# Identity matmuls on TensorE while it waits at the start of a graph-attention layer

## The chip, the cores and the metric

The kernel runs on one core of a Trainium2 chip. The metric is the device time of one execution in microseconds; a measurement is the median of a few executions. TensorE (PE) multiplies matrices, VectorE (DVE), ScalarE (ACT) and GpSimd (POOL) do the element-wise work, and SyncE (SP) issues most of the DMAs. Each engine runs its own list of instructions in order and waits on semaphores that others raise.

## The reference

One layer of masked attention and an MLP over 128 graphs of 64 nodes, 512 channels, 8 heads, everything in float32:

```
nx = layernorm(x, ln1_g, ln1_b)
q, k, v = nx @ Wq + bq, nx @ Wk + bk, nx @ Wv + bv          # 512 x 512 each
scores = where(adj, q k^T / 8, -1e9);  attn = softmax(scores)
x = x + (attn v) @ Wo + bo
nx = layernorm(x, ln2_g, ln2_b)
return x + gelu(nx @ W1 + b1) @ W2 + b2                     # 512 -> 2048 -> 512
```

## The kernel before

The 8192 tokens are worked off in 16 groups of 512 tokens (4 tiles of 128). The first phase does the attention group by group. The second phase does the MLP over 8 super groups of 1024 tokens. Float32 products of the linear layers are split into three matmuls of a rounded type (`split3`, lines 180 to 182): weights and activations each have a high part (`w_hi`, `nxT_hi`) and a low part (`w_lo`, `nxT_lo`), and hi*lo, lo*hi and hi*hi are summed in PSUM. Each of these matmuls has 512 columns. Scores, attention outputs and transposes use plain float32 operands.

The start is written out by hand, and the change is there. Every engine has a list of its own for it:

- GpSimd fills the 128x128 identity matrix `ident` (lines 530 to 533) and raises `ident_done`.
- SyncE loads the four tiles of the first group of `x`, then `Wq` in four parts, `Wk`, `Wv`, the second group of `x` and the first mask.
- VectorE takes statistics of one tile after another (line 936 and after it), GpSimd takes the power that gives the reciprocal root (line 666), and VectorE normalizes the tile (line 957), raising `zn_done`.
- TensorE waits for `ident_done`, then for each tile for `zn_done`, and transposes its four 128x128 blocks with the identity (line 1539), 16 transposes in all, into four PSUM banks that are otherwise those of the scores and of the transposed probabilities. The last tile's four raise `t_done` one by one.
- ScalarE turns each of the four transposed blocks into `z1T` (scale and bias, line 700) and rounds it to `nxT_hi` (line 707). VectorE subtracts to get `nxT_lo` (line 980) and raises `nx_split`. ScalarE also rounds the weights (lines 689 and 887), and the low parts of the weights are made by VectorE (lines 927 and 1292) and, for `Wk`, by GpSimd (line 661).
- TensorE then makes the queries of the first group (`first_queries`): for each of 4 chunks of the channels it waits for `nx_split` and issues 12 matmuls of 512 columns, 48 in all, into the four banks `lin[0]` to `lin[3]`. After them it makes the keys, which need `wk_lo`, the values, which need `wv_lo`, and the transposes of the second group (line 1351).

After the start, TensorE's work follows `ORDER`, a hand-written list for one group of the first phase: S are scores (line 1398), P transposes of probabilities (line 1408), O attention outputs (line 1425), W output projections, U linear units of the next group. The last group has a list of its own, `LAST_ORDER`, in which the first products of the MLP stand between pieces of attention; around 790 and 817 us the trace is in the last two groups.

In PSUM, `lin` has `LIN` = 4 banks of 128 x 512 float32. The first matmul of each accumulation group overwrites its bank (start=True).

Of the kernel before, what the change touches and what calls it, by code (L numbers as in the profile page):

```python
# [38 lines left out]
P = 128  # L39
# [7 lines left out]
TILES = 4  # L47
# [23 lines left out]
LIN = 4  # L71
# [41 lines left out]
def order_of(g):  # L113
    if isinstance(g, int) and g < 0:
        units = [("U", j) for j in FIRST_UNITS]
        return units[:-3] + [("T", k) for k in range(KC)] + units[-3:] if g == -1 else []
    if is_last(g):
        return LAST_ORDER
    if isinstance(g, int) and g == NG - 2:

        return [("S", 0), ("U", 0), ("U", 1), ("U", 3), ("P", 0), ("U", 4), ("U", 6), ("S", 1), ("O", 0), ("U", 7), ("W", 0),
                ("P", 1), ("U", 9), ("O", 1), ("W", 1), ("U", 10), ("W", 2), ("W", 3)]
    return [(k, n) for k, n in ORDER if k in kinds_of(g)]
# [38 lines left out]
def is_first(g):  # L162
    return isinstance(g, int) and g == 0
# [21 lines left out]
def adj_layer(nc, x_dram, adj, ln1_g, ln1_b, ln2_g, ln2_b, wq, bq, wk, bk, wv, bv, wo, bo, w1, b1, w2, b2, out_dram):  # L185
# [10 lines left out]
    with ctx:  # L196
# [8 lines left out]
        ident = sb("ident", [P, P])  # L205
# [15 lines left out]
        start = nc.sbuf_base  # L221
# [66 lines left out]
        with ExitStack() as phase:  # L288
            lin_banks = phase.enter_context(nc.psum_tensor("lin", [P, LIN, GT], F32))
            lin = [lin_banks[:, i] for i in range(LIN)]  # L290
# [1036 lines left out]
        def _(pe):  # L1327
            def take_bank(g, kind, n):

                bank, last = ring_place(g, kind, n)  # L1330
                if last is not None:
                    i, kind, n = last
                    which = {"U": (q_done, k_done, v_done)[n % 3], "L": v_done, "T": nx_done, "O": att_split,
                             "W": x1_done}[kind]
                    if kind == "L":
                        pe.wait_ge(v_done, KC * i + n // 3 + 1)
                    elif kind == "U":
                        pe.wait_ge(which, KC * (i + 1) + n // 3 + 1)
                    elif kind == "T":
                        pe.wait_ge(which, KC * (i + 2) + n + 1)  # L1340
                    elif kind == "O":
                        pe.wait_ge(which, PAIRS * i + n // 2 + 1)
                    else:
                        pe.wait_ge(which, TILES * i + n + 1)
                return lin[bank]

            def transposes(g, par, k, bank):

                pe.wait_ge(zn_done, TILES * (g + 1))
                for t in range(TILES):  # L1350
                    mm = pe.transpose(bank[:, t * P:(t + 1) * P], x[par][:, t, k * P:(k + 1) * P], ident[:, :])
                mm.then_inc(t_done, 1)

            def unit(g, j, bank):

                m, which = j // 3, j % 3
                if is_first(g) and m == 0:
                    pe.wait_ge(w_lo_done[which], 1)
                for c in range(KC):
                    if j == 0:  # L1360
                        pe.wait_ge(nx_split, KC * g + c + 1)
                    nx = (nxT_hi[:, c, :], nxT_lo[:, c, :])
                    if which < 2:
                        lhs = tuple(w[which][:, c, m * P:(m + 1) * P] for w in (w_hi, w_lo))
                        rhs = nx
                    else:
                        lhs = tuple(n[:, m * P:(m + 1) * P] for n in nx)
                        rhs = tuple(w[2][:, c, :] for w in (w_hi, w_lo))
                    mm = split3(pe, bank[:, :], lhs, rhs, c == 0, c == KC - 1)
                mm.then_inc(u_done, 1)  # L1370
# [13 lines left out]
            def score(g, par, u):  # L1384


                n = PAIRS * g + u
                if u == 0:
                    pe.wait_ge(q_done, KC * (g + 1))
                    pe.wait_ge(k_done, KC * (g + 1))  # L1390
                wait_apart(pe, masked, n, s_passed)
                for t in range(2):
                    for m in range(KC):
                        for a in range(2):
                            at = (2 * u + t) * P + a * NODES
                            for h in range(2):
                                rows = slice(h * HD, (h + 1) * HD)
                                mm = pe.matmul(ps_scores[a * NODES:(a + 1) * NODES, h * KC + m, t, :],
                                               qT[par][rows, m, at:at + NODES], kT[par][rows, m, at:at + NODES],
                                               start=True, stop=True)  # L1400
                mm.then_inc(s_done, 1)

            def prob_transposes(g, u):
                n = PAIRS * g + u
                pe.wait_ge(prob_done, n + 1)
                wait(pe, probT_done, 4 * n)
                for h in range(HEADS):
                    mm = pe.transpose(ps_probT[:, h, :], prob[:, h, :, :], ident[:, :])
                mm.then_inc(pt_done, 1)
# [29 lines left out]
            def body(g, par):  # L1439
                for kind, n in order_of(g):  # L1440
                    if kind == "S":
                        score(g, par, n)
                    elif kind == "P":
                        prob_transposes(g, n)
                    elif kind == "F":
                        product(0, 0, n)
                    elif kind == "L":
                        unit(g, n, take_bank(g, "L", n))
                    elif kind == "U":
                        if is_first(g + 1) and n % 3 == 0:  # L1450
                            if n == 0:
                                first_queries()
                        else:
                            unit(g + 1, n, take_bank(g, "U", n))
                    elif kind == "O":
                        attend(g, par, n, [take_bank(g, "O", 2 * n + a) for a in range(2)])
                    elif kind == "W":
                        project(g, n, take_bank(g, "W", n))
                    else:
                        transposes(g + 2, par, n, take_bank(g, "T", n))  # L1460


            def product(s, q, i):

                n = NQ * s + q
                if i == 1:
                    pe.wait_ge(w1_loaded[q % 2], 16 * (NQ // 2 * s + q // 2 + 1))
                if q == 0:
                    pe.wait_ge(conv_split, PROD * s + CONV.index(i) + 1)
                first_step = isinstance(s, int) and s == 0 and q == 0  # L1470
                if i == 1:
                    if first_step:
                        pe.wait_ge(masked, PAIRS * NG)
                    else:
                        pe.wait_ge(gelu_done["C21"], n)
                elif i == 2:
                    if first_step:
                        pe.wait_ge(probT_done, 4 * PAIRS * NG)
                    else:
                        pe.wait_ge(c_added["C11"], n)  # L1480
                elif i == 5:
                    if not first_step:
                        pe.wait_ge(c_added["C12"], n)
                elif i == 3:
                    pe.wait_ge(c_added["C22"], n + 1)
                else:
                    pe.wait_ge(snap_done[{6: 0, 7: 1, 4: 2}[i]], n + 1)
                for c in range(2):
                    mm = split3(pe, ps_of[i][:, :],
                                tuple(w1_ring[:, q % 2, part, W_AT[i], c * P:(c + 1) * P] for part in range(2)),  # L1490
                                tuple(nxc[:, NX_AT[i], part, c] for part in range(2)),
                                c == 0 and i in (1, 2, 5), c == 1, i not in (1, 2, 5))
                mm.then_inc(p_done[i], 1)
# [39 lines left out]

            pe.wait_ge(ident_done, 1)

            for t in range(TILES):
                pe.wait_ge(zn_done, t + 1)
                for k in range(KC):
                    mm = pe.transpose(first_t[k][:, t * P:(t + 1) * P], x[0][:, t, k * P:(k + 1) * P],
                                      ident[:, :])  # L1540
                    if t == TILES - 1:
                        mm.then_inc(t_done, 1)
            body(-1, 1)
            body(0, 0)
            with pe.Fori(1, NG - 4, 2) as g:
# [36 lines left out]
```

## Time and profile before

| | us |
|---|---|
| median of 3 executions | 2147.41 |
| lowest and highest of them | 2147.28, 2148.95 |
| the profiled execution, whole | 2148.58 |
| its span, first to last instruction on the core | 2146.6 |
| TensorE busy in the span | 2125.0 |
| VectorE busy | 1490.7 |
| ScalarE busy | 905.0 |

The profiled execution is 1.17 us above the median, and 1.98 us of it lie outside the span. All times below are from the start of the span. In the timeline, a matmul's duration includes its way through the engine, so neighbouring matmuls overlap; what tells the pace of a stream is the distance from one start to the next.

### The profile page before, as it was taken

The page shows a single profiled execution, that of the slowest core. Times are in us where ns is not written, and L with a number is a line of the kernel's source. Part 1 is how long each engine was busy: PE and PEld are TensorE (multiplying, and loading weights), DVE is VectorE, ACT ScalarE, POOL GpSimd, SP SyncE. Part 2 cuts the span into 40 slices and gives each one's busy share as a digit, 9 for nine tenths or more (in the row PEclk, how much of TensorE's full clock was granted, in tenths as well). Part 3 has the DMA queues.
Part 4 walks back from the last instruction along what each step waited for, and adds up shares of the span by engine and source line. Part 5 has one row for each costly group of instructions (what it writes and reads, how often), then busy time and mean ns, then how long its engine had stood idle before and what let it go on. Part 6 is the DMA issues. An engine that isn't in the chain of part 4 may idle for free.

```text
span 2146.6 us, 33138 instructions
## 1 busy us (share of the span) xinstructions
PE 2125.0 (99%) x13216; PEld 1754.3 (82%) x13216; DVE 1490.7 (69%) x2211; ACT 905.0 (42%) x1321; POOL 431.6 (20%) x293
## 2 busy tenths in 40 slices
PE   8999999999999999999999999999999999999999
PEld 6888888888888877888888888888888888888887
DVE  5888888888999966666666666666666656666333
ACT  4444444433344444435335335335345345345332
POOL 2233434321111224004004004003003003003200
PEclk9999999999999999999999999999999999999999
DMA  6344333431222116336445445444444544544532
GB/s 188 111 155 135 134 134 134 146 117 66 70 76 70 46 56 231 150 140 223 170 156 206 168 173 190 177 181 179 187 181 171 196 180 167 201 165 172 211 129 92
DMA packets 103842, 323.98 MB, mean 151 GB/s; under 512 B 21409, under 2 KB 29601, under 8 KB 87329
## 3 DMA queue, kind: packets, MB, share of 16 engines
q1 hardware_dynamic: 98192, 321.68, 40.9%
q8 instruction: 85, 1.39, 0.3%
q10 hardware_dynamic: 5520, 0.55, 0.2%
q14 instruction: 45, 0.36, 0.1%
HBM read 265.57 MB, written 56.62 MB: 150 GB/s over the span
## 4 chain that ended last, share of the span: by engine, by line
PE 96%; DVE 3%; DMA 0%; ACT 0%; issue 0%; POOL 0%; SPq 0%; DVEq 0%; ACTq 0%
PE lin L180 11%; PE lin L182 10%; PE lin L181 10%; PE ps_r L180 5%; PE ps_r L182 5%; PE ps_r L181 5%; PE ps_x L180 5%; PE ps_x L182 5%; PE ps_out L182 5%; PE ps_x L181 5%; PE ps_out L181 5%; PE ps_out L180 5%; PE ps_z L182 3%; PE ps_z L181 3%; PE ps_z L180 3%; PE lin L1425 1%
## 5 line engine op out<-in xcount | busy, mean ns | idle before, releaser
L1209 DVE TENSOR_TENSOR acc<-ps_r,acc 128x512 f32<-128x512 f32 x256 | 176.4, 689 | 329.7 <-PE ps_r L182 329.0
L817 ACT ACTIVATE snaps<-ps_x 128x512 f32<-128x512 f32 x192 | 114.3, 596 | 410.1 <-PE ps_x L182 410.0
L180 PE MATMUL ps_r<-w_ring,h_ring 128*128 128x512 f32 x512 | 199.5, 390 | 0.7 <-DVE h_ring L1199 0.6
L180 PE MATMUL ps_x<-nxc,w_ring 128*128 128x512 f32 x512 | 199.4, 389 | 0.0
L181 PE MATMUL ps_x<-nxc,w_ring 128*128 128x512 f32 x512 | 199.2, 389 | 0.0
L182 PE MATMUL ps_r<-w_ring,h_ring 128*128 128x512 f32 x512 | 199.2, 389 | 0.0
L182 PE MATMUL ps_x<-nxc,w_ring 128*128 128x512 f32 x512 | 199.2, 389 | 0.0
L181 PE MATMUL ps_r<-w_ring,h_ring 128*128 128x512 f32 x512 | 199.2, 389 | 0.0
L180 PE MATMUL ps_out<-w_ring,h_ring 128*128 128x512 f32 x512 | 199.2, 389 | 0.0
L182 PE MATMUL ps_out<-w_ring,h_ring 128*128 128x512 f32 x512 | 199.2, 389 | 0.0
L181 PE MATMUL ps_out<-w_ring,h_ring 128*128 128x512 f32 x512 | 199.2, 389 | 0.0
L547 POOL TENSOR_TENSOR xres<-xres,bo_all 128x512 f32<-128x512 f32 x64 | 85.7, 1349 | 429.2 <-DMA xres<-in_x 427.6
L964 DVE STREAM_TRANSPOSE z1T<-x 32x512 f32<-32x512 f32 x224 | 157.5, 703 | 5.3
L964 DVE STREAM_TRANSPOSE bT<-xb 32x512 f32<-32x512 f32 x224 | 157.3, 702 | 4.3
L826 ACT ACTIVATE hf_a<-hf_a,b_cols 128x512 f32<-128x512 f32 x128 | 92.7, 725 | 150.4 <-DVE hf_a L1194 150.4
L1199 DVE TENSOR_TENSOR h_ring<-hf_b,h_ring 128x512 fp32r<-128x512 f32 x128 | 91.2, 712 | 49.3 <-ACT h_ring L833 49.1
L645 POOL TENSOR_TENSOR rstd<-var_eps,minus_half 128x4 f32<-128x4 f32 x14 | 19.4, 1385 | 499.1 <-DVE var_eps L1165 499.1
L180 PEld LDWEIGHTS ps_r<-w_ring,h_ring 128*128 128x128 f32 x512 | 96.1, 188 | 21.6 <-issue 1.7
L181 PEld LDWEIGHTS ps_out<-w_ring,h_ring 128*128 128x128 f32 x512 | 96.1, 188 | 20.0
L180 PEld LDWEIGHTS ps_x<-nxc,w_ring 128*128 128x128 f32 x512 | 96.1, 188 | 20.0
L181 PEld LDWEIGHTS ps_x<-nxc,w_ring 128*128 128x128 f32 x512 | 96.1, 188 | 20.0
L180 PEld LDWEIGHTS ps_out<-w_ring,h_ring 128*128 128x128 f32 x512 | 96.1, 188 | 19.9
(137 smaller groups left out, 5056.7 us busy)
## 6 DMA issues: line engine op xcount, KB each, us to landing
w_ring<-w_scratch SPq DMA_DIRECT2D x64, 1792.0 KB, 7.3
w_ring<-w_scratch SPq DMA_DIRECT2D x64, 1024.0 KB, 7.1
xb<-x_scratch SPq DMA_DIRECT2D x22, 1024.0 KB, 10.1
xres<-in_x SPq DMA_DIRECT2D x64, 256.0 KB, 3.4
x_scratch<-xres SPq DMA_DIRECT2D x64, 256.0 KB, 2.1
x<-in_x SPq DMA_DIRECT2D x15, 1024.0 KB, 6.0
acc<-x_scratch SPq DMA_DIRECT2D x32, 256.0 KB, 2.9
out<-xb SPq DMA_DIRECT2D x32, 256.0 KB, 2.0
```

Source lines behind the costliest of these rows:

```text
L180: pe.matmul(out, lhs[1], rhs[0], start=first, stop=False, skip_group_check=resumed)
L181: pe.matmul(out, lhs[0], rhs[1], start=False, stop=False, skip_group_check=resumed)
L182: return pe.matmul(out, lhs[0], rhs[0], start=False, stop=last, skip_group_check=resumed)
L547: pool.tensor_tensor(xres[:, t % 2], xres[:, t % 2], bo_all[:, :], ALU.add).then_inc(xres_biased, 1)
L645: pool.tensor_tensor(rstd[:, :], var_eps[:, :], minus_half[:, :], ALU.pow).then_inc(m_rstd_done, 1)
L817: act.activation(snaps[:, j], ps_x[:, :], ACT.Copy).then_inc(snap_done[j], 1)
L826: act.activation(hf[c], ps_x[:, :] if c == "C21" else hf[c], ACT.Gelu, bias=b1_cols[:, m:m + 1]).then_inc(gelu_done[c], 1)
L964: return dve.transpose(to[channels, :, :].rearrange("p k (t n) -> p t k n", n=P)[:, :, :, tokens], source[tokens, :, :].rearrange("p t (k ...
L1199: dve.tensor_tensor(h_ring[:, n % 2, 1, at], hf[c], h_ring[:, n % 2, 0, at].bitcast(F32), ALU.subtract).then_inc(h_split[c], 1)
L1209: dve.tensor_tensor(acc(t), ps_r[:, :], acc(t), ALU.add).then_inc(acc_added, 1)
L1425: mm = pe.matmul(banks[a][rows, out:out + NODES], v[par][keys, 2 * u + t, head * HD:(head + 1) * HD], probT[keys, t, h * KC + m, :], start ...
```

## The change

Before the first tile, after each of the first three tiles, and after the last tile, TensorE multiplies the identity by itself, into the first 128 columns of the bank `lin[3]`, which no one reads before the first queries overwrite it. There are 14, then 2 + 2 + 2, then 8 of these matmuls, 28 in all. They wait for nothing but `ident_done` and raise no semaphore. No other engine's list changes, and no other instruction of TensorE moves against another.

```diff
             pe.wait_ge(ident_done, 1)
 
+            def keep_going(count):
+
+                for _ in range(count):
+                    pe.matmul(lin[LIN - 1][:, :P], ident[:, :], ident[:, :], start=True, stop=True)
+
+            keep_going(14)
             for t in range(TILES):
                 pe.wait_ge(zn_done, t + 1)
                 for k in range(KC):
@@
                     if t == TILES - 1:
                         mm.then_inc(t_done, 1)
+                keep_going(2 if t < TILES - 1 else 8)
             body(-1, 1)
             body(0, 0)
```

## Rows read from the trace of the kernel before

**Rows 1.** The page: busy time by engine, and the chain that ended last

```profile
PE 2125.0 (99%) x13216; PEld 1754.3 (82%) x13216; DVE 1490.7 (69%) x2211; ACT 905.0 (42%) x1321; POOL 431.6 (20%) x293
...
PE 96%; DVE 3%; DMA 0%; ACT 0%; issue 0%; POOL 0%; SPq 0%; DVEq 0%; ACTq 0%
```

**Rows 2.** Whom TensorE waited for: total us, times, longest

```profile
PE ps_scores L1539 <- DVE x L957: 7.6, 3, 6.9
```

**Rows 3.** Timeline 0:15: start, duration, engine line op tiles, count [idle before <-releaser]

```profile
1.22 0.29 POOL L533 TENSOR_SCALAR_AFFINE_SELECT ident<-ident 128x128 f32<-128x128 f32 x1 [0.24 <-POOL minus_half L531]
...
6.91 0.66 PE L1539 MATMUL ps_scores<-ident,x 128*128 128x128 f32 x2 [6.91 <-DVE x L957]
...
8.34 0.69 PE L1539 MATMUL ps_scores<-ident,x 128*128 128x128 f32 x2 [0.35 <-DVE x L957]
...
9.81 0.69 PE L1539 MATMUL ps_scores<-ident,x 128*128 128x128 f32 x2 [0.35 <-DVE x L957]
10.29 0.63 PE L1539 MATMUL ps_probT<-ident,x 128*128 128x128 f32 x2
10.79 0.69 PE L1539 MATMUL ps_scores<-ident,x 128*128 128x128 f32 x2
...
11.37 0.78 ACT L700 ACTIVATE z1T<-ps_scores,cols 128x512 f32<-128x512 f32 x1 [0.89 <-PE ps_scores L1539]
...
13.68 0.77 PE L180 MATMUL lin<-nxT_hi,wq_lo 128*128 128x512 f32 x1 [1.77 <-DVE nxT_lo L980]
```

**Rows 4.** Timeline of TensorE, 18:28, in the first queries and at the first key

```profile
18.51 0.63 PE L182 MATMUL lin<-nxT_hi,wq_hi 128*128 128x512 f32 x1
18.94 0.47 PE L180 MATMUL lin<-nxT_hi,wq_lo 128*128 128x512 f32 x1
19.25 0.40 PE L181 MATMUL lin<-nxT_lo,wq_hi 128*128 128x512 f32 x1
...
27.20 0.39 PE L180 MATMUL lin<-nxT_hi,wk_lo 128*128 128x512 f32 x1
```

**Rows 5.** Windows, 12:19: length, then PE, PEld, DVE, ACT, POOL busy; PEclk, DMA, GB/s

```profile
16.00:19.00 3.00, 3.00 (x9) 2.32 (x8) 1.39 (x2) 2.97 (x3) 0.00 (x0) 1.00 1.08 358
```

**Rows 6.** Timeline 40:53: transposes of the second group, scores, a first matmul after idling

```profile
40.81 1.91 PE L1351 MATMUL lin<-ident,x 128*128 128x128 f32 x16
...
42.47 0.47 PE L180 MATMUL lin<-wv_hi,nxT_lo 128*128 128x512 f32 x1
...
50.83 1.16 PE L1398 MATMUL ps_scores<-kT,qT 64*64 64x64 f32 x64
...
52.50 0.47 PE L180 MATMUL lin<-nxT_hi,wq_lo 128*128 128x512 f32 x1 [0.51 <-DVE nxT_lo L980]
52.80 0.39 PE L181 MATMUL lin<-nxT_lo,wq_hi 128*128 128x512 f32 x1
```

**Rows 7.** Timeline 17:33: what the first queries, the keys and the values wait for

```profile
17.35 0.69 DVE L980 TENSOR_TENSOR nxT_lo<-z1T,nxT_hi 128x512 fp32r<-128x512 f32 x1 [0.64 <-ACT nxT_hi L707]
...
19.19 4.62 POOL L661 TENSOR_TENSOR wk_lo<-v,wk_hi 128x2048 fp32r<-128x2048 f32 x1 [9.04 <-ACT wk_hi L689]
...
21.15 4.81 DVE L927 TENSOR_TENSOR wv_lo<-softmax,wv_hi 128x2048 fp32r<-128x2048 f32 x1 [3.11 <-ACT wv_hi L689]
```

**Rows 8.** Windows, 790:796: columns as in Rows 5

```profile
790.00:792.00 2.00, 1.51 (x4) 1.22 (x5) 0.44 (x1) 1.98 (x5) 0.52 (x1) 0.62 0.33 129
...
794.00:796.00 2.00, 2.00 (x10) 1.67 (x9) 0.00 (x0) 0.82 (x1) 2.00 (x1) 1.00 0.20 75
```

**Rows 9.** Timeline of TensorE, 785:819, around its long waits in the last two groups

```profile
788.21 1.16 PE L1425 MATMUL lin<-probT,v 64*64 64x64 f32 x64 [2.03 <-ACT probT L731]
790.49 0.79 PE L180 MATMUL lin<-wo_hi,attT_lo 128*128 128x512 f32 x1 [1.13 <-DVE xres L1029]
...
793.65 0.52 PE L181 MATMUL lin<-wo_lo,attT_hi 128*128 128x512 f32 x1
...
816.45 1.09 PE L1408 MATMUL ps_probT<-ident,prob 128*128 128x128 f32 x8 [2.33 <-DVE prob L1013]
```

## The prediction

> **What bounds the kernel now.** I read the busy times and the chain of the page first: TensorE is busy in 2125.0 of 2146.6 us and makes up 96% of the chain that ended last [rows 1]. So time can come only from TensorE's few idle stretches or from work that it does slower than it could. The list of its waits comes next: 7.6 us go to the normalized tiles of the first group, 6.9 of them before the first [rows 2], and 1.77 us to the first `nxT_lo` [rows 3]. The change fills these waits; it does not shorten them, since what ends them is on VectorE, ScalarE and DMA. What it can change is the pace of what follows, and that is in the timeline. The first queries start at 13.68 us [rows 3], the twelfth matmul of them at 18.51, the thirteenth at 18.94, the fourteenth at 19.25 [rows 4]. The eleven steps from 13.68 to 18.51 take 4.83 us, 0.44 us each with the start in it, and the next takes 0.43. From 19.25 to 27.20 there are 35 steps in 7.95 us, 0.227 us each. The same shape runs at nearly half the pace until about 19.0 us. 512 columns in 0.43 us is the lower of the clock's two levels, 1.2 GHz. The column of the granted clock does not say so, it reads 1.00 in that stretch [rows 5]; but later in the trace it does: it drops to 0.62 after 790 us, and is 1.00 again from 794 [rows 8]. I take the pace as the witness at the start, the column later. So TensorE is at its lower level for the first 5.3 us of unbroken work.
>
> **The change part by part.**
>
> *Price of one identity matmul.* No row shows a plain float32 matmul of 128x128. Nearest are two. The 16 transposes at the full clock start over 42.47 - 40.81 = 1.66 us, 0.104 each [rows 6]; at the lower level two take 10.29 - 9.81 = 0.48, 0.24 each [rows 3]. One score unit is 32 matmuls in the code and 64 in the trace, so a plain float32 matmul is two records. Two records at a transpose's pace give 0.21 us at the full clock and 0.45 at the lower. From the other side, those 32 matmuls of 64x64 take 1.16 us [rows 6], 0.036 each; an identity matmul has four times the blocks and twice the columns, 8 x 0.036 = 0.29, and 0.55 to 0.6 at the lower level. I take 0.21 and 0.45, because shape and partition count are the transposes'. The Trainium skill, "FP8 and Floating Point Precision", section "TensorE Precision Notes", states that true FP32 makes four passes through the array; by it an identity matmul would be 4 x 128 columns, an estimate of 0.43 us at 1.2 GHz and 0.21 at 2.4, and the sum would be the same as by the lower end.
>
> *The 14 before the first tile.* `ident` is ready at 1.51 us, the first tile's transpose starts at 6.91 [rows 3], a cover of 5.3 us. All 14 at the lower level would take 6.3 us (8.1 at the dear end) and hold that transpose up by 0.9 to 2.7 us. But if the clock rises on the way they are shorter. It rose 5.3 us after the dense stream began at 13.68; around 790 us the slow stretch lasted from 790.49 to about 793.8, inside the last matmul that is still longer than 0.39, 3.3 us [rows 9]. So I expect the rise between 1.6 + 3.3 = 4.9 and 1.6 + 5.3 = 6.9 us. With 6.9: 11.8 matmuls are done by then, 2.2 x 0.21 = 0.5 remain, they end at 7.4. The first tile is 0.5 us late.
>
> *The tiles.* That lateness does not last. The tiles start at 6.91, 8.34, 9.81 and 10.79 [rows 3]. At the full clock, four transposes and two identity matmuls need 0.42 + 0.42 = 0.84 us. The second tile would start at 8.34 as now, the third at 9.81 and end, with its pair, at 10.65, before the last at 10.79. At the dear end (0.29) it is 10.81, hardly late. ScalarE began `z1T` 0.58 us after the start of the last tile's first transpose; at the full clock that transpose is 0.13 shorter in pace and somewhat more in latency. Worth 0.1 to 0.3 us; I take 0.15.
>
> *The 8 after the last tile.* They start at 10.79 + 0.42 = 11.2 and take 1.7 us (2.3), until 12.9 to 13.5. The first `nxT_lo` lets TensorE go at 13.68, or 0.15 sooner. Hidden; the cover is 0.1 to 0.6 us thin. At the lower level they would take 3.6 us and end at 15.3 or later.
>
> *What is gained.* At the full clock, a first matmul after idling is followed after 0.30 us (52.50 to 52.80, [rows 6]), the rest after 0.227. The first to the fourteenth would take 0.30 + 12 x 0.227 = 3.02 instead of 19.25 - 13.68 = 5.57 us: 2.55 us. What is late next? The fourth chunk of `nxT_lo` ends at 18.04 and is then wanted at 13.68 + 0.30 + 35 x 0.227 = 21.9. `wk_lo` ends at 23.81 on GpSimd and would be wanted at 27.20 - 2.55 - 0.15 = 24.5, a margin of 0.7. `wv_lo` ends at 25.96 [rows 7], ten us ahead of the values. From there VectorE and ScalarE wait for TensorE's units, and all of it moves as one. Sum: 2.55 + 0.15 = 2.7 us, from 2148.58 to 2145.9 for the profiled execution. The median is 1.17 lower. Some of that may be a shorter slow stretch at the start, since its end hung on when the clock rose, and then there is less to win. I take 0.3 off for it: 2147.41 - 2.4 = **2145.0**.
>
> **The rivals.**
>
> *The gain is lost or doubled further on.* Near 788 us TensorE waited 2.03 and then 1.13 us with 1.16 us of work between, and near 814 it waited 2.33 us [rows 9]; after the first the granted clock fell for some 3.3 us [rows 8], about 1.65 us of it lost at half the pace. With all of it 2.5 us earlier, a fall may come at another moment, fail to come, or come once more. For it: the three executions lie 1.67 us apart, just one such stretch. Against it as a systematic effect: the gaps themselves stay. By one fall more or less it gives 2145.0 plus or minus 1.65, so 2143.4 to 2146.7.
>
> *The clock rises and falls back before the queries.* Between the 14 and the 8, TensorE does only transposes and six identity matmuls, 1.3 us of them from 7.4 to 11.2, no more than the 1.16 us of matmuls between the two waits before the fall at 790 [rows 9]. 16 transposes ran from 6.91 to about 11.9 and the level at 13.68 was yet the lower, but 1.77 us of idling lie between [rows 3], so the trace does not decide whether transposes hold a clock up. If they don't, it could fall around 10 to 12 us; then the last 8 run slow in part and the queries start up to 1.5 us late and slow. The gain shrinks to between 0 and 1 us, time 2146.4 to 2147.4. Against it: TensorE's waits from 7.4 to 13.6 would be 0.6 us at the longest. The Trainium skill, "TensorE: Matmul & The Clock Gate", section "Part 4: PE-mode transpose", says that transposes do not count as busy for the clock in the way that matmuls do, which speaks for this rival.
>
> *Slower.* If identity matmuls do not lift the clock, everything stays at the lower level and the fill is on the path: the 14 end at 1.6 + 6.3 = 7.9, each of four tiles takes 0.96 and each pair 0.9. The first tile ends at 8.9 and its pair at 9.8, the second's pair at 11.6, the third's at 13.5, the last tile's transposes run 13.5 to 14.4, 2.7 us late, and the 8 until 18.0, 4.3 us after 13.68. With the slow stretch as now that is 2147.4 + 4.3 = 2151.7; at the dear end (0.57) 8.5 us. The point from which the change loses is a rise later than about 9 us: then the tiles fall behind. Against it: every plain stream of matmuls in the trace is fast after 5.3 us at most.
>
> *The change does nothing.* If the clock came up near 19 us for a reason of its own (the time since the start), the pace of the queries would stay, and only the fill's delay of the last rival would come on top: 2147.4 to 2151.7. Against it: it fell and rose again at 790, so it follows the work.
>
> **How the numbers follow.** The forecast with its scatter from the falls near 790 and 817 us has 0.83; a clock that falls back before the queries 0.08; the rise stays at 19 us 0.04; slower by the fill 0.05. The forecast's own range is 2143.4 to 2146.7. To leave no more than 2 in 10 out, I keep its low end and reach into the second rival: 2143.4 to 2147.2. A measurement of this kernel can tell about 0.2% from no change, 4.3 us. Faster than 2143.1 needs the full gain and an episode less: 0.05. Slower than 2151.7 is the dear half of the third rival: 0.03. Within 0.2%: 0.92.
>
> **What the profile of the changed kernel would show.** The identity matmuls should appear as 56 records, the first at about 1.6 us, with steps of about 0.2 us per record that halve between 4.9 and 6.9. The transposes of the last tile should still start at about 10.8 and be half as far apart. The first query should start within 0.2 us of 13.6 with steps of 0.227 at once, the first key at about 24.5. The prediction is wrong if the first key is not at least 2 us earlier than 27.20, if the last tile's transposes start after 11, or if a wait on `wk_lo` shows; and its way to the end is wrong if the first key is early and the end is not.

## The result: slower by 0.7%, and not where the change was made

| | before | after |
|---|---|---|
| median, us (6 executions each) | 2147.35 | 2162.97 |
| lowest, highest | 2146.23, 2148.95 | 2161.63, 2163.46 |
| span of the profiled execution | 2146.6 | 2161.4 |

The ratio is 1.0072, with a 95% interval from 1.0059 to 1.0085. The forecast was 2145.0 us, the range ended at 2147.2.

**The start did what was forecast.** The timeline of TensorE in the kernel after, against [rows 3] and [rows 4]:

```profile
1.56 6.31 PE L1539 MATMUL lin<-ident 128*128 128x128 f32 x28 [1.56 <-POOL ident L533]
7.70 0.39 PE L1545 MATMUL ps_scores<-ident,x 128*128 128x128 f32 x2
...
8.14 0.61 PE L1539 MATMUL lin<-ident 128*128 128x128 f32 x4
8.59 0.38 PE L1545 MATMUL ps_scores<-ident,x 128*128 128x128 f32 x2
...
10.96 0.44 PE L1545 MATMUL ps_scores<-ident,x 128*128 128x128 f32 x2
...
13.70 0.47 PE L180 MATMUL lin<-nxT_hi,wq_lo 128*128 128x512 f32 x1 [0.30 <-DVE nxT_lo L980]
14.01 0.39 PE L181 MATMUL lin<-nxT_lo,wq_hi 128*128 128x512 f32 x1
14.24 0.40 PE L182 MATMUL lin<-nxT_hi,wq_hi 128*128 128x512 f32 x1
...
24.70 0.39 PE L180 MATMUL lin<-nxT_hi,wk_lo 128*128 128x512 f32 x1
```

The queries run at steps of 0.23 us from the first on, and the first key comes at 24.70 instead of 27.20: 2.50 us earlier.

**A part of that is gone 25 us later.** Before, TensorE waited 0.51 us at 52.50 for the first `nxT_lo` of the second group [rows 6]. After, it waits 1.60 at 51.08. The second row is VectorE's four instructions of that line (durations: least, median, most). The third is GpSimd's timeline after, the fourth the same additions before:

```profile
51.08 0.47 PE L180 MATMUL lin<-nxT_hi,wq_lo 128*128 128x512 f32 x1 [1.60 <-DVE nxT_lo L980]
```

```profile
L980 DVE TENSOR_TENSOR nxT_lo<-z1T,nxT_hi x4: 678/680/1784, 49.2 to 52.1; 128x512 fp32r<-128x512 f32 x4
```

```profile
47.88 2.51 POOL L547 TENSOR_TENSOR xres<-xres,bo_all 128x512 f32<-128x512 f32 x2 [16.89 <-DMA xres<-in_x]
```

```profile
49.24 2.54 POOL L547 TENSOR_TENSOR xres<-xres,bo_all 128x512 f32<-128x512 f32 x2 [18.29 <-DMA xres<-in_x]
```

One of the four took 1.78 us where the others take 0.68, while GpSimd added biases. Before, the additions ended at 51.78, and the first subtraction began at 51.66, so the two hardly met.

**The rest happens in the loop of the first phase.** This loop is entered once and jumps back five times. Its first work is a score unit, 64 records. In the kernel before:

```profile
202.51 1.16 PE L1398 MATMUL ps_scores<-kT,qT 64*64 64x64 f32 x64
...
303.29 1.16 PE L1398 MATMUL ps_scores<-kT,qT 64*64 64x64 f32 x64
```

The same places in the kernel after, and ahead of them the first entry into the loop:

```profile
100.22 1.16 PE L1398 MATMUL ps_scores<-kT,qT 64*64 64x64 f32 x64
...
201.02 0.65 PE L1398 MATMUL ps_scores<-kT,qT 64*64 64x64 f32 x27
203.99 0.80 PE L1398 MATMUL ps_scores<-kT,qT 64*64 64x64 f32 x37 [2.32 <-issue]
...
304.50 0.65 PE L1398 MATMUL ps_scores<-kT,qT 64*64 64x64 f32 x27 [0.16 <-issue]
307.49 0.89 PE L1398 MATMUL ps_scores<-kT,qT 64*64 64x64 f32 x37 [2.35 <-issue]
```

"issue" means that nothing the profile shows held the engine up. All five jumps look alike: 27 records, 1.8 to 2.4 us of nothing, 37 records. On the first entry, from above and not by a jump, the same 64 records ran through. The list of TensorE's waits has the idling as its first line; before, the same line stood at 0.2 us:

```profile
PE ps_scores L1398 <- issue: 11.1, 6, 2.3
```

```profile
PE ps_scores L1398 <- issue: 0.2, 1, 0.2
```

After two of the idle stretches the granted clock falls too. The window 308:312 (length, then busy time of PE, PEld, DVE, ACT, POOL; clock, DMA share, GB/s):

```profile
308.00:312.00 4.00, 4.00 (x29) 3.12 (x20) 3.41 (x3) 0.00 (x0) 0.00 (x0) 0.57 0.93 310
```

Where the time went, by the start of the same instruction in both timelines:

| | before | after | difference | added in between |
|---|---|---|---|---|
| first key | 27.20 | 24.70 | -2.50 | -2.50 |
| loop entered | 101.66 | 100.22 | -1.44 | +1.06 |
| jump 1 | 202.51 | 201.02 | -1.49 | 0 |
| jump 2 | 303.29 | 304.50 | +1.21 | +2.70 |
| jump 3 | 404.21 | 409.32 | +5.11 | +3.90, one fall of the clock |
| jump 4 | 504.88 | 514.10 | +9.22 | +4.11, one fall of the clock |
| jump 5 | 605.51 | 617.31 | +11.80 | +2.58 |
| half a round later | 655.82 | 669.73 | +13.91 | +2.11 |
| end of the span | 2146.6 | 2161.4 | +14.8 | +0.9 |

A queue that loads instructions shows five packets more, as many as there are jumps back (packets, MB, share; first before, then after):

```profile
q8 instruction: 85, 1.39, 0.3%
```

```profile
q8 instruction: 90, 1.47, 0.3%
```

### The profile page after: what moved, and what is told of

Its sections match the earlier page's. It is cut to its first block, busy times and chain, and to the rows that moved or that the text cites. A ratio compares the mean times of both kernels' runs of the same rounds, so it can differ in the third digit from the quotient of the medians.

```text
span 2161.4 us, 33249 instructions
## 1 busy us (share of the span) xinstructions
PE 2133.7 (99%) x13272; PEld 1763.7 (82%) x13272; DVE 1492.9 (69%) x2211; ACT 904.2 (42%) x1321; POOL 432.7 (20%) x293
## 4 chain that ended last, share of the span: by engine, by line
PE 95%; DVE 3%; issue 1%; ACT 0%; DMA 0%; POOL 0%; SPq 0%; DVEq 0%; ACTq 0%
PE lin L180 10%; PE lin L181 10%; PE lin L182 10%; PE ps_r L180 5%; PE ps_r L181 5%; PE ps_r L182 5%; PE ps_x L180 5%; PE ps_x L182 5%; PE ps_x L181 5%; PE ps_out L180 5%; PE ps_out L182 5%; PE ps_out L181 5%; PE ps_z L182 3%; PE ps_z L180 3%; PE ps_z L181 3%; PE ps_scores L1398 1%
## 5 line engine op out<-in xcount | busy, mean ns | idle before, releaser
L711 ACT ACTIVATE qT<-lin,cols 128x512 f32<-128x512 f32 x64 | 44.1, 689 | 176.1 <-PE lin L182 176.0
L180 PEld LDWEIGHTS ps_r<-w_ring,h_ring 128*128 128x128 f32 x512 | 96.1, 188 | 22.2 <-issue 2.4
L182 PEld LDWEIGHTS ps_r<-w_ring,h_ring 128*128 128x128 f32 x512 | 96.1, 188 | 20.0
```

What stands on the lines that cost most here:

```text
L180: pe.matmul(out, lhs[1], rhs[0], start=first, stop=False, skip_group_check=resumed)
L182: return pe.matmul(out, lhs[0], rhs[0], start=False, stop=last, skip_group_check=resumed)
L711: act.activation(qT[par][:, m, :], lin[bank][:, :], ACT.Identity, bias=cols[:, 2, m:m + 1]).then_inc(q_done, 1)
```

## The experiments

The change adds 28 plain float32 matmuls ahead of the loop, and that is 56 records. If a record is a weight load and a matmul, the code of the loop lies 112 instructions further on.

**Theory A:** the place of the loop in TensorE's instruction stream is the cause. Instructions come in blocks. After a jump back the first block is there when it is needed, but the next one starts to load with the jump and takes some 3 us. How long the first block lasts depends on where in it the loop begins. **Theory B:** the earlier start, or what the identity matmuls do to clock, memory or other engines, is the cause. In the runs a loop is placed with an argument that says at which slot of a block of 256 its first instruction stands. Runs with it have line numbers that are one to fifteen higher. The ratio given with each run is the one on record; it differs from the quotient of the two medians by at most 0.0004.

The Trainium skill, "Runtime: NRT & Kernel Launch", section "Instruction fetch mechanics", states that instructions are fetched in blocks of 16 KiB, which is 256 instructions, and that a jump breaks the fetching ahead. The block's size agrees with the trace: each of the 85 packets above has 16,384 bytes.

### The shift alone, the identity matmuls alone

`shift_only` is the kernel before with

```diff
-            with pe.Fori(1, NG - 4, 2) as g:
+            with nc.Fori(1, NG - 4, 2, engines=OrderedEngineSet([pe.engine]), head_slot={pe.engine: 198}) as g:
```

> The kernel before, without identity matmuls; only the place of the first-phase loop of TensorE in its stream of instructions is changed: its first instruction is put at slot 198 of a block of 256 instructions, which is where 27 records of the first score unit (54 instructions, and 4 at the head) run before the block ends, as in the changed kernel. Theory A (the loss is the code's place: after each of the 5 jumps back TensorE runs out of loaded instructions at the end of the first block): idle of about 2.3 us after 27 score records in each of 5 rounds, with falls of the clock in some, 10 to 15 us slower than before: 2157 to 2162. Theory B (the loss comes from the earlier start or from what the identity matmuls do to clock, memory or the other engines): no idle after 27 records, time within 1 us of before, 2147.

Measured: 2163.79 us against 2148.12, ratio 1.0077 (1.0062 to 1.0092). The whole loss is there without one identity matmul, and at 15.7 us it is just beyond the 10 to 15 that were expected. Its first two jumps back:

```profile
202.62 0.67 PE L1399 MATMUL ps_scores<-kT,qT 64*64 64x64 f32 x27
205.06 0.80 PE L1399 MATMUL ps_scores<-kT,qT 64*64 64x64 f32 x37 [1.77 <-issue]
...
305.43 0.65 PE L1399 MATMUL ps_scores<-kT,qT 64*64 64x64 f32 x27
308.18 0.80 PE L1399 MATMUL ps_scores<-kT,qT 64*64 64x64 f32 x37 [2.10 <-issue]
```

`warm_at_86` is the changed kernel with the same line and slot 86.

> The changed kernel with all 28 identity matmuls, with the loop's first instruction put at slot 86, 112 instructions (28 x 4) earlier in the block than I reckon for the changed kernel, so where the kernel before should have it. Theory A: no idle inside the score unit after the jumps back, the first loop starts 1.4 us earlier than before (100.2 instead of 101.7) and all of the 1.4 us arrives at the end: 2146.0, plus or minus one fall of the clock (1.7). Theory B: 2160 to 2163 as the changed kernel.

Measured: 2146.81 us against 2148.12, ratio 0.9995 (0.9986 to 1.0004). No idle over 0.2 us is left at the jumps, and the loop is entered at 99.78. Theory B falls: each half of the change was run without the other. The gain of the identity matmuls by themselves is too small for this measurement to tell from none.

`before_at_86` is the control, the kernel before with slot 86.

> The kernel before with its loop's head put at slot 86, where it should be already. Control of the count and of what putting it there costs: the same time as before within 0.5 us, no idle at the jumps beyond 0.2 us, first loop at 101.7. If the slot was another, or placing it costs a jump over padding, it is up to 3 us slower.

Measured: 2147.15 against 2147.70, ratio 0.9997 (0.9988 to 1.0006). No idle over 0.2 us at the jumps; placing the loop costs nothing that shows.

### How much of the block is left

`shift_128` is the kernel before with slot 128.

> The kernel before with the loop's first instruction at slot 128. Now 124 instructions behind the head of 4 (62 records of the score unit, 1.1 us instead of 0.65) run before the block ends. Theory A with a fixed fetch time of about 3 us after the jump: idle of about 1.85 us instead of 2.3 after 62 score records, 5 times, 9 to 12 us slower than before. If the place matters only as near or far from the loop's head, without a fixed time, the idle would be 0 or 2.3. Theory B: no change.

Measured: 2160.4, ratio 1.0061 (1.0046 to 1.0076). Two of its jumps:

```profile
201.83 1.15 PE L1399 MATMUL ps_scores<-kT,qT 64*64 64x64 f32 x62
204.25 0.32 PE L1399 MATMUL ps_scores<-kT,qT 64*64 64x64 f32 x2 [1.27 <-issue]
...
406.65 1.15 PE L1399 MATMUL ps_scores<-kT,qT 64*64 64x64 f32 x62
409.72 0.33 PE L1399 MATMUL ps_scores<-kT,qT 64*64 64x64 f32 x2 [1.92 <-issue]
```

The place is met to the record. From slot 198 to 128 are 70 instructions; the idle moved from after record 27 to after record 62, 35 records. And the work goes on at about the same time after the first score in all three slow kernels: 2.47 to 2.99 us in the changed kernel, 2.42 to 3.03 with slot 198, 2.23 to 3.07 with slot 128, fifteen jumps in all. The idle is what is left of that time when the block has run out. I had expected 1.85 us, and it was 1.1 to 1.9.

The trace has the block itself. Its list of DMA packets has, at each of these fifteen jumps, one instruction packet of 16,384 bytes that starts between 0.06 us before the first score and 0.76 us after it, and takes 0.9 to 1.4 us. TensorE goes on 1.20 to 1.54 us after that packet's end, every time. Three of the fifteen, in us from the first score:

| | packet starts | packet ends | work goes on | after the packet's end |
|---|---|---|---|---|
| changed kernel, jump 1 | 0.27 | 1.65 | 2.97 | 1.32 |
| slot 198, jump 3 | 0.76 | 1.63 | 3.02 | 1.39 |
| slot 128, jump 5 | -0.06 | 0.88 | 2.23 | 1.35 |

The kernels without idle have this packet at the same place (in the kernel before at 0.19 us after the first score of jump 1, until 1.48), but their first block lasts longer. And it isn't the five packets more that cost the time: with slot 128 there are 85 packets, as before, and the idle is there. From one jump to the next the changed kernel loads ten blocks, the kernel before nine. A round has 1911 weight loads and matmuls, so by estimate it reaches into a ninth block from slot 198, and ends in the eighth from 86 and, just, from 128.

`warm_at_104` is the changed kernel with slot 104.

> Identity matmuls, loop at slot 104. 148 instructions behind the head of 4 run before the block ends: the 64 score records and 10 matmuls of 512 columns, so the end comes about 3.5 us after the first score. The fetch has ended 2.4 to 3.1 us after the first score in every round seen. Theory A: no idle at all after the jumps, time equal to slot 86 within 1 us. If the cost grows evenly with the distance from slot 86, there would be about 0.4 us per round, 2 us in all.

Measured: 2145.98, ratio 0.9994 (0.9985 to 1.0003), no idle over 0.2 us. So the cost does not grow evenly: it was 12 us with slot 128 and nothing that shows with slot 104, where the first block should last some 3.5 us (an estimate, from the run's expectation) and the work behind it was possible after 3.1 at the latest.

`warm_hint` leaves the loop where the changed kernel has it and puts one instruction at its head that names the jump at its end, `hint_back_edge=True`.

> The changed kernel with a prefetch hint for the jump back at the head of the first-phase loop (one more instruction per round), loop left where it falls (slot 198 or 199). If the idle is the fetch of the loop's first block, the hint starts it earlier and takes most of the 11 us away: 2148 to 2151. If it is the fetch of the block behind the first one, which starts only after the jump, the hint takes nothing away: 2160 to 2163. Theory B: 2160 to 2163.

Measured: 2146.1, ratio 0.9993 (0.9984 to 1.0002), no idle after the score records. I had said that a hint would do nothing if the second block was the late one. It was, and the hint removed all of it. The loop does lie where it lies in the changed kernel: up to the first jump back its instruction packets come at the same times after the entry into the loop, to 0.3 us. With the hint a round loads nine blocks instead of ten, and the packet near the jump starts 1.0 us after the first score and ends at 2.0 to 2.9. By the lag above that is too late for a block that is wanted after 27 records, so the block behind the target was there already. Which packet brought it is open.

The same section of the Trainium skill states that a jump to a block that isn't loaded has to wait for that block. No run here shows such a wait: 27 or 62 records ran at once, with 0.2 us of idling before them at most. But in every kernel a packet starts 2.8 to 3.3 us before the first score of a jump, while TensorE works. It may be the target's block, loaded in time; the trace doesn't say. What had to be waited for was the block behind it.

### The microsecond at 50 us

`warm_86_pool_waits` has slot 86 and one more wait on GpSimd, so that its two additions come after VectorE's subtractions.

```diff
+                if g == 0:
+                    pool.wait_ge(nx_split, 2 * KC)
                 bias_xres(g, 0)
                 bias_xres(g, 1)
```

> Identity matmuls, loop at slot 86, and GpSimd waits for the fourth nxT_lo of the second group before it adds the output bias to the first two residual tiles. In the changed kernel the first nxT_lo of that group took 1.78 us on VectorE instead of 0.69, and TensorE waited 1.60 us; GpSimd's two additions ran at that time. Theory C (the two engines hold each other up, and this eats 1.1 of the 2.5 us): the four nxT_lo take 0.69 each, TensorE waits about 0.5 us, the first loop starts at 98.9 instead of about 99.9 to 100.2, and the end is 1.1 us earlier than with slot 86 alone. Rival D (the long nxT_lo has another cause, such as a late ScalarE or a DMA): it stays 1.5 to 1.8 us long and nothing moves.

Measured: 2144.82 against 2147.89, ratio 0.9989 (0.9980 to 0.9998). VectorE's four subtractions take 0.68 to 0.69 us again, TensorE's wait is back at 0.51, as in [rows 6], and the loop is entered at 99.02 instead of 99.78: of the 2.5 us nothing is lost there any more.

```profile
49.89 0.47 PE L181 MATMUL lin<-nxT_hi,wq_lo 128*128 128x512 f32 x1 [0.51 <-DVE nxT_lo L983]
...
99.02 1.16 PE L1401 MATMUL ps_scores<-kT,qT 64*64 64x64 f32 x64
```

Theory C holds by the trace: TensorE's part moved by 2.5 us and GpSimd's, which waited for a load, by 1.4 (49.24 to 47.88), and so they met. In the medians this step is not clear of noise: its interval overlaps that of `warm_at_86`. Why VectorE is held up no run shows.

### Which identity matmuls are needed

`only_first_14` has slot 86 and leaves out the fill between and after the tiles:

```diff
             keep_going(14)
...
-                keep_going(2 if t < TILES - 1 else 8)
```

> Only the 14 identity matmuls before the first tile; none between the tiles and none after them; loop at slot 86. From 7.7 us TensorE does only the 16 transposes and then waits 1.8 to 2 us for the first nxT_lo. If transposes hold the clock up, the first queries are 0.227 us apart from the start and the first key comes at 24.7 as with all 28. If transposes do not hold it, the clock falls between 8 and 13.7 us, the queries start 0.43 us apart for up to 5 us, and the first key comes between 26 and 27.2.

Measured: 2147.15, ratio 0.9998 (0.9989 to 1.0008). The transposes ran at the full clock, but after 2.08 us of waiting the first query was slow again, and the first key came at 27.39:

```profile
13.61 0.76 PE L181 MATMUL lin<-nxT_hi,wq_lo 128*128 128x512 f32 x1 [2.08 <-DVE nxT_lo L981]
14.17 0.63 PE L182 MATMUL lin<-nxT_lo,wq_hi 128*128 128x512 f32 x1
```

```profile
10.00:14.00 4.00, 1.58 (x9) 1.14 (x10) 3.58 (x6) 3.36 (x7) 0.23 (x1) 0.84 1.04 386
14.00:18.00 4.00, 4.00 (x10) 3.05 (x10) 2.14 (x4) 3.94 (x6) 0.00 (x0) 0.50 1.07 379
```

So 14 matmuls at the head alone are worth nothing that shows; it takes fill between or behind the tiles to carry the clock over. This run leaves out both; `five_wide` below, with none between them and a little behind, tells more.

`transposes_instead` replaces each identity matmul by two transposes of the identity, slot 86.

> 56 transposes of the identity in place of the 28 identity matmuls (one record instead of two each, so the same number of instructions), at the same places; loop at slot 86. If transposes lift the clock as matmuls do, their distance falls from 0.24 to 0.10 us between 4.9 and 7 us, and the first key comes at 24.7. If they don't, they stay 0.21 to 0.24 apart, the 28 before the first tile end at about 8 us, the last tile's transposes start 1 to 2 us late, the queries start slow at 14 to 16 us and the first key comes at 28 to 29: 1 to 2 us slower than before.

Measured: 2146.72, ratio 0.9994 (0.9984 to 1.0003), first key at 24.33. No matmul but transposes ran before 13.36, and TensorE was at its upper level:

```profile
1.56 5.37 PE L1540 MATMUL lin<-ident 128*128 128x128 f32 x28 [1.56 <-POOL ident L534]
6.77 0.38 PE L1546 MATMUL ps_scores<-ident,x 128*128 128x128 f32 x2
6.99 0.38 PE L1546 MATMUL ps_probT<-ident,x 128*128 128x128 f32 x2
...
13.36 0.47 PE L181 MATMUL lin<-nxT_hi,wq_lo 128*128 128x512 f32 x1 [0.34 <-DVE nxT_lo L981]
13.66 0.40 PE L182 MATMUL lin<-nxT_lo,wq_hi 128*128 128x512 f32 x1
```

The first of them start 0.21 us apart, and from 5.9 us on it is 0.11 (two tile transposes from 6.77 to 6.99). The column of the granted clock reads 1.00 in 2 to 6 us too, so the pace is the witness. Float32 transposes lift the clock as matmuls do. The rule that the prediction cited against this (the Trainium skill, "TensorE: Matmul & The Clock Gate", "Part 4: PE-mode transpose") does not hold in this run, whose pace went from 0.21 to 0.11 us, and the measurement decides.

### Two more versions

`five_wide` puts 5 wide identity matmuls in the place of 28 small ones, 3 before the first tile and 2 after the last, and leaves the loop alone.

```diff
-                    pe.matmul(lin[LIN - 1][:, :P], ident[:, :], ident[:, :], start=True, stop=True)
+                    pe.matmul(lin[LIN - 1], ident[:, :], ident[:, :].unsqueeze(1).broadcast_to((P, KC, P)), start=True, stop=True)
```

> 5 identity matmuls of 512 columns instead of 28 of 128 (3 before the first tile, none between the tiles, 2 after the last), the loop left where it falls. They are 20 instructions instead of 112, so by my count the loop's head falls on slot 106 instead of 198, and 146 instructions run before the block ends. Theory A: no idle after the jumps back, first key near 24.7, 2146 plus or minus 1.7, as with all 28 at slot 86 or 104. If the clock needs the pairs between the tiles, the first key comes near 27 and the time is that of before; if the count is off, idle of up to 1 us after each jump, 2148 to 2152.

Measured: 2146.01, ratio 0.9993 (0.9984 to 1.0003), first key at 25.00, no idle over 0.2 us at the jumps. Each expectation was met in part: the clock did fall between the tiles (the last figure but two of the rows below, 0.89 and 0.50), and it was up again right after the first query, which was still slow: 0.58 us to the second, then 0.23. So 2.2 of the 2.5 us at the queries come without the pairs between the tiles. In the median no gain is clear of noise.

```profile
8.00:10.00 2.00, 0.80 (x5) 0.57 (x6) 1.73 (x5) 1.42 (x3) 1.32 (x2) 0.89 1.04 384
10.00:12.00 2.00, 2.00 (x9) 1.73 (x10) 1.76 (x4) 1.05 (x2) 0.20 (x1) 0.50 1.05 393
```

`warm_and_fill_late` adds to `warm_86_pool_waits` the same trick at the two long waits of [rows 9], where the clock fell in the kernel before. It also puts the loop of the MLP at slot 0 of a block:

```diff
+                if is_last(g) and u == 0:
+                    pe.wait_ge(probT_done, 4 * n)
+                    keep_going(9, ps_probT[:, 0, :])
                 pe.wait_ge(prob_done, n + 1)
...
+                if isinstance(g, int) and g == NG - 2 and u == 1:
+                    keep_going(8, banks[0][:, :P])
                 wait_apart(pe, probT_done, 4 * (PAIRS * g + u + 1), o_passed)
```

> As the run with identity matmuls, loop at slot 86 and GpSimd's wait, and besides: 8 identity matmuls before TensorE waits for the second transposed probabilities of the last group but one (near 786 us), 9 before it waits for the first probabilities of the last group (near 814 us), into banks that the matmuls behind them overwrite; the loop of the MLP phase at slot 0 of a block. Theory (the clock falls there because TensorE idles 2.0 and 2.3 us, and each fall costs half of 3.3 us): no window near 790 and 820 reads a granted clock under 1.0, and the time is 1.7 to 3.3 us lower than without the fill: 2142 to 2143. If the falls are hidden behind VectorE's chain there, the clock stays up and the time is the same, 2144.8.

Measured: 2143.78 against 2147.70, ratio 0.9982 (0.9973 to 0.9991), the fastest of all, and the one whose gain over the kernel before is clearest. The stretch around 790 us, first in `warm_86_pool_waits`, then with the fill:

```profile
786.00:790.00 4.00, 2.89 (x21) 2.23 (x14) 1.23 (x3) 2.33 (x5) 1.69 (x1) 0.53 0.19 70
790.00:794.00 4.00, 4.00 (x13) 3.10 (x12) 0.03 (x1) 1.03 (x1) 3.92 (x3) 0.62 0.22 66
```

```profile
786.00:790.00 4.00, 2.94 (x13) 2.44 (x14) 0.98 (x2) 2.34 (x5) 1.95 (x1) 1.00 0.17 66
790.00:794.00 4.00, 4.00 (x19) 3.19 (x18) 1.82 (x2) 2.19 (x3) 3.92 (x3) 1.00 0.20 72
```

The clock reads 1.00 there and at 812 to 820 us, and as the mean of the whole span in all eleven executions. The two versions ran against different runs of the kernel before, so the step from 0.9989 to 0.9982 is not shown by itself; the medians are 1.0 us apart, less than the 1.7 to 3.3 expected, and the spans of the profiled executions 3.1 (2144.1 and 2141.0). The part of the MLP's loop in it wasn't run alone.

## Why the prediction was wrong, point by point

- **The price of an identity matmul was right.** 14 of them took 7.70 - 1.56 = 6.14 us, 0.44 each, all at the lower level; a pair at the full clock took 8.59 - 8.14 = 0.45, 0.22 each. Forecast: 0.45 and 0.21.
- **The rise was later than its range** of 4.9 to 6.9 us in this execution: all of the 14 ran slow, and the pace doubled at 7.7 us. In seven other kernels that begin with such a fill it came at 4.5 to 7.3 us. The first tile was 0.8 us late, and the tiles caught up as forecast: the last began at 10.96 against 10.79. The extra 0.15 us from there did not come.
- **The gain at the queries was right**: 2.50 us against 2.55. `wk_lo` was no wait, and none of the signs at the start by which the prediction would be wrong came. The one on its way to the end did: the first key was early and the end was not.
- **"From there ... all of it moves as one" failed first.** GpSimd's additions hung on a load and not on TensorE, moved by 1.4 us instead of 2.5, and met the subtraction that TensorE waits for: 1.06 us. The prediction had looked for engines that would be late, and not for two that would be busy at once.
- **What a change adds to the code was priced only as time on the engine, and this is the step that decided.** The prediction said of the 28 matmuls where they lie in time, not that the loop behind them would lie 112 instructions further on. None of its rivals named it. It was a term put at nothing. It cost 15.4 us between jump 1 and the middle of the last round: 11.0 of idle in TensorE's rows, about 3 by two falls of the clock that followed it, and most of the rest in restarting (at jump 1 the first matmul behind the scores comes 3.70 us after the first score instead of 1.10, which is 2.60 more, with 2.32 of idle in it). The last 0.9 us of the table, up to the end of the span, no run explains.
- **Its range and chances** (0.92 for within 0.2%) rested on the belief that a fill of 6 us has effects of that order. The rivals that were named were all among those 6 us; none of them came. One of their sums is off: 28 identity matmuls at 0.57 and 16 transposes at 0.24 us from 1.6 on end 7.7 us after 13.68, not 8.5, which takes 0.6 for one.
- **The rival on transposes** was wrong in its ground, and right in its outcome for another kernel: without the fill between and behind the tiles the clock falls (`only_first_14`), because TensorE waits and not because it transposes: with transposes as fill and waits of 0.37 us at most it stayed up.

## What to carry to other kernels

Ahead of a loop whose instructions are loaded anew in every round (here nine or ten packets a round), every added or removed instruction is also a change of where the loop lies, and it is paid at every jump back if the loop begins with many short instructions and its first block runs out before the next one is there. Look for "issue" in the list of waits after any edit; place the loop, hint the jump, or make the addition in few, wide instructions: each of the three left no such idle here. When one engine is made earlier, ask which others stay, and what will now be busy at the same time.

## What was not expected of the hardware

- The block behind a jump's target was there 2.2 to 3.1 us after the first score, in 15 jumps. A score record takes 0.018 us, so one block of 128 of them would last 2.3 us, less than most of these fetches; with 512-column matmuls at 0.227 us a block lasts 29 us (both are estimates from these paces).
- The MLP's loop lies 112 instructions further on too, and no wait over 0.15 us shows on TensorE between 1100 and 2000 us. Between 1200 and 1950 us the changed kernel loads not one block by that queue, while a super group takes some 160 us (an estimate: eight in 1310 us). So that loop stays loaded over its jumps, and the loop of the first phase does not.
- A TensorE idle of 1.8 to 2.4 us may be followed by 3.3 us at half the clock, or not: two of five in the changed kernel, two of five with slot 198. The cost of an idle stretch thus comes with a scatter of about 1.6 us.
- A chain of float32 transposes alone brought TensorE to its upper level, and held it through the tiles, with waits of 0.36 and 0.37 us in between.
